# A fifth batch in seven block products: batch 4 of a conditioned two-layer residual kernel, with rank products and operand sums moved ahead

## The chip, the cores and the metric

The kernel runs on one core of a Trainium2 chip. The metric is device time in microseconds, the median of three runs. The profile is one further execution of the same program.

## The reference

Eight batches of x (1024 rows of 512) go through two layers, each with a residual. The first layer adds to its weight a product of rank 8 that is made from the batch's condition vector; the second scales its input columns by the condition and its output columns by a norm.

```python
xw = h @ w2 + b2                       # h = gelu(layernorm(cond) @ w1 + b1), a vector per batch
x_a, x_b = split(xw, 2)                # each (b, 512, 8)
layer = base_layer + einsum('bdr,bkr->bdk', x_a, x_b)
x = x + (x + einsum('btc,bco->bto', x, layer))
ys = cond / sqrt(512)
d = rsqrt(einsum('bi,io->bo', ys * ys, weight * weight) + 1e-8)
x = x + einsum('bsi,io->bso', x * ys, weight) * d
```

The two layers are linear in x, so per batch they are one 512 x 512 matrix, P, applied to x.

## The kernel before, in words

**Precision.** Each fp32 operand is held as two fp32r parts, high (rounded, copied by ScalarE: `x_high`, `q_high`, `r_high`) and low (the rest, subtracted by VectorE: `x_low`, `q_low`, `r_low`). A product takes three matmuls: high by high, high by low, low by high. All matmuls meant here are 128 x 128 by 128 x 512.

**P.** For batch b, P is base^T (w0, fixed) times a right factor r (built from w1, `ys` and `dinv` of the batch, by `r_scale`, `r_eye`, `r_high`, `r_low`, four chunks each) plus a product of rank 8 by 16 rows ("rank product", `rank`, one matmul for each of four chunks). Batches 0, 1 and 3 have their base tiles made early; 2 and 4 are made together as a pair in seven block products. All five are stored in `base` without the rank product, which TensorE writes to the four banks `ranks`, and VectorE adds it there (`p_sum`). For batches 5, 6 and 7 TensorE makes P late: four late tiles (`late_base`) of 12 matmuls and one rank product each, in the same four banks, between other work; ScalarE copies them out (`keep_late`). `rank_free` keeps TensorE from writing one of those banks before what was in it has been read: for a stored batch it waits for `p_summed` of the batch before.

**Applying P.** A plain batch takes two halves (h) of four tiles (o), each tile 4 x 3 matmuls over the chunks cc, so 96. A fast batch (those in `FAST`) is one Strassen-Winograd product: seven block products, the steps j of `STEPS`, each two tiles m of six matmuls, so 84. It needs from each operand four extra sums: of x (`x_sums_first`: three of them, t1, t3, t2; `x_sums_last`: t4), of P, called q here, (s1, s3, s2, s4). VectorE makes all of them. On the way out ScalarE evacuates banks 0 and 1 (`evacuate_block`, parts a, b, c, c12) and VectorE adds banks 2 and 3 (`finish_block`, blocks c11, c22, c21). A plain batch is evacuated by ScalarE alone. A bank is written anew only when it was read: `given` names for each step the block or part that must be out; step 6 waits for c22.

**Order.** Each engine runs its instructions in the order written; nothing else plans. While TensorE applies P to batch b, ScalarE and VectorE make the operands of batch n = b + 1 (`plain_batch`, `fast_batch` and, between two fast batches, `fast_pair`, in each engine's block). Buffers are rings: four slots for split x operands (`X_RING`), eight for q (`Q_RING`), six raw buffers for loaded quarters of x and the sum t2 (`RAW`). A slot is written when the matmuls of its former operand are done. SP's queue issues the loads of x (`load_x`) and some of the stores, in an order written out by hand; ScalarE's queue issues the other stores. GpSimd makes the masked left side of the rank products (`amk`, two buffers).

**Lines of the profile.** L1464 matmuls of a plain batch, L1495 of a fast one, L1323 late tiles, L1309 rank products; on VectorE L1000 low parts of x, L1069 low parts of q, L1012 to L1021 the sums of x, L1058 P's sums, L1105 `finish_block`, L930 a sum in the pair's preparation; on ScalarE L537 high parts of x, L566 high parts of q, L591 and L606 evacuations, L713 a scaling of r.

## Time and profile before

| | |
|---|---|
| median of 3 runs | 287.53 us (287.08 to 288.37) |
| profiled execution: device time | 287.95 us |
| its span, first to last instruction | 286.2 us |
| TensorE with work | 281.4 us, 98% |
| VectorE busy | 228.1 us, 80% |
| ScalarE busy | 170.1 us, 59% |
| granted TensorE clock, mean | 0.999 |

Matmuls are pipelined, and one's duration in the trace (0.39 us) is longer than the distance to the next. So TensorE's time is read from starts: where instructions of a line are merged, their number and the start of the next line give the distance. Durations of neighbouring VectorE instructions overlap a little in the same way. The time in brackets in an order of time is how long the engine was idle before the line, and for whom.

### The profile page before, as it was taken

Reading aid. Unit: us, or ns where it says so; the run is one execution under the profiler, and the core shown is the slowest. Engines: PE = TensorE matmul, PEld = TensorE weight load, DVE = VectorE, ACT = ScalarE, POOL = GpSimd, SP = SyncE. Lnnn points to the kernel's source line nnn. Section 1 sums busy time; section 2 is a strip of 40 time slices with the busy share of each in tenths; the row PEclk is TensorE's granted clock in tenths of the full one; section 3 lists DMA queues with packets and bytes.
Section 4 is the critical chain, followed back from the end, with each engine's and each line's share of the span. In section 5 each row is a group of like instructions: output and inputs, shape, how many; then the busy total and the mean of one; then the engine's idle time right before and its main releaser. Section 6 shows DMA issues by size and latency. Waiting matters only on the chain.

```text
span 286.2 us, 3812 instructions
## 1 busy us (share of the span) xinstructions
PE 281.4 (98%) x1368; PEld 222.0 (78%) x1368; DVE 228.1 (80%) x341; ACT 170.1 (59%) x260; POOL 18.6 (6%) x35
## 2 busy tenths in 40 slices
PE   8999999999999999999999999999999999999994
PEld 8778374756788888888888888888888888888783
DVE  3979969936688999984899978766787998987972
ACT  4757865530653648863648865534785587743771
POOL 5000000000520211000211000020000000000000
PEclk9999999999999999999999999999999999999999
DMA  6999797978044113499313499201134152371105
GB/s 187 372 425 422 290 421 297 419 302 324 2 147 147 76 74 128 165 279 407 123 79 142 149 301 419 89 0 74 73 114 182 74 179 116 101 266 73 53 23 220
DMA packets 13697, 55.31 MB, mean 193 GB/s; under 512 B 1776, under 2 KB 1776, under 8 KB 11376
## 3 DMA queue, kind: packets, MB, share of 16 engines
q1 hardware_dynamic: 10800, 45.64, 42.7%
q10 hardware_dynamic: 2880, 9.44, 8.3%
q8 instruction: 11, 0.18, 0.3%
q14 instruction: 6, 0.05, 0.1%
HBM read 38.30 MB, written 16.78 MB: 192 GB/s over the span
## 4 chain that ended last, share of the span: by engine, by line
PE 98%; DVE 0%; issue 0%; POOL 0%; POOLq 0%
PE tile L1495 33%; PE tile L1464 23%; PE tile L1384 7%; PE aux L1323 6%; PE acc L1255 5%; PE tile L1287 4%; PE tile L1270 4%; PE tile L1430 4%; PE spare L1323 3%; PE acc L1323 3%; PE tile L1226 2%; PE aux L1309 1%; PE aux L1233 1%; PE aux L1400 1%; PE spare L1309 1%; PE acc L1309 1%
## 5 line engine op out<-in xcount | busy, mean ns | idle before, releaser
L1495 PE MATMUL tile<-xs,qs 128*128 128x512 f32 x420 | 97.4, 390 | 0.0
L1495 PEld LDWEIGHTS tile<-xs,qs 128*128 128x128 f32 x420 | 78.7, 188 | 17.0 <-issue 0.7
L1464 PE MATMUL tile<-xs,qs 128*128 128x512 f32 x288 | 68.2, 389 | 0.0
L1464 PEld LDWEIGHTS tile<-xs,qs 128*128 128x128 f32 x288 | 54.1, 188 | 11.2
L1000 DVE TENSOR_TENSOR xs<-stream,xs 128x1024 fp32r<-128x1024 f32 x33 | 40.0, 1221 | 10.3 <-ACT xs L537 10.0
L537 ACT CAST xs<-stream 128x1024 fp32r<-128x1024 f32 x33 | 34.3, 1049 | 4.3 <-ACT stream L591 1.9
L606 ACT ACTIVATE stream<-tile,dts 128x512 f32<-128x512 f32 x40 | 26.6, 687 | 12.3 <-PE tile L1495 12.1
L591 ACT ACTIVATE stream<-tile,dts 128x512 f32<-128x512 f32 x24 | 16.4, 688 | 27.9 <-PE tile L1464 27.9
L1069 DVE TENSOR_TENSOR qs<-base,qs 128x512 fp32r<-128x512 f32 x38 | 25.0, 685 | 4.1 <-ACT qs L566 4.1
L1105 DVE SCALAR_TENSOR_TENSOR stream<-tile,dts,stream 128x512 f32<-128x512 f32 x30 | 21.9, 747 | 6.1 <-PE tile L1495 4.3
L417 POOL TENSOR_SCALAR amk<-asq,mask 128x512 fp32r<-128x512 f32 x8 | 14.3, 1794 | 172.9 <-PE spare L1309 98.9
L566 ACT CAST qs<-base 128x512 fp32r<-128x512 f32 x38 | 22.3, 620 | 4.3 <-DVE base L1165 1.9
L433 ACT CAST rs<-rtmp 128x512 fp32r<-128x512 f32 x24 | 14.7, 620 | 12.1 <-DVE rtmp L830 11.9
L1000 DVE TENSOR_TENSOR xs<-xr,xs 128x1024 fp32r<-128x1024 f32 x14 | 17.0, 1221 | 4.0 <-ACT xs L537 3.9
L1323 PE MATMUL aux<-rs,w0s 128*128 128x512 f32 x72 | 17.3, 389 | 0.0
L835 DVE TENSOR_TENSOR rs<-rtmp,rs 128x512 fp32r<-128x512 f32 x24 | 16.5, 687 | 0.8 <-ACT rs L433 0.4
L1323 PEld LDWEIGHTS aux<-rs,w0s 128*128 128x128 f32 x72 | 13.5, 188 | 2.8
L537 ACT CAST xs<-xr 128x1024 fp32r<-128x1024 f32 x14 | 14.6, 1049 | 0.5 <-ACT stream L606 0.5
L1430 PE MATMUL tile<-rs,w0s 128*128 128x512 f32 x48 | 12.1, 393 | 0.0
L1270 PE MATMUL tile<-rs,w0s 128*128 128x512 f32 x48 | 12.0, 401 | 0.0
L1287 PE MATMUL tile<-rs,w0s 128*128 128x512 f32 x48 | 11.5, 394 | 0.1
L1287 PEld LDWEIGHTS tile<-rs,w0s 128*128 128x128 f32 x48 | 8.9, 188 | 3.1 <-issue 1.3
(170 smaller groups left out, 324.2 us busy)
## 6 DMA issues: line engine op xcount, KB each, us to landing
...
```

The costliest lines, as they stand in the source:

```text
L537: nc.scalar.copy(x_slot(b, x)[:, 0], x_raw(b, home)).then_inc(x_hi, 1)
L566: nc.scalar.copy(to, src).then_inc(p_hi, 1)
L606: nc.scalar.activation(pairs[:, slot, m], tiles[m][:], ACT.Copy, scale=dts[:, b, o:o + 1]).then_inc(bank_free, 1)
L1000: nc.vector.tensor_tensor(x_slot(b, x)[:, 1], x_raw(b, home), x_slot(b, x)[:, 0].bitcast(F32), ALU.subtract).then_inc(x_lo, 1)
L1069: nc.vector.tensor_tensor(to, src, hi, ALU.subtract).then_inc(p_lo, 1)
L1105: nc.vector.scalar_tensor_tensor(to, tiles[2 + m][:], dts[:, b, o:o + 1], to, ALU.mult, ALU.add).then_inc(block_out, 1)
L1270: last = nc.tensor.matmul(tiles[cc][:], w0s[:, u, kc, cc * P:(cc + 1) * P], rs[:, kc, v], start=kc == 0 and (u, v) == (0, 0), stop=kc == K ...
L1287: last = nc.tensor.matmul(tiles[cc][:], w0s[:, u, kc, cols], rs[:, kc, v], start=kc == 0 and (u, v) == (0, 0), stop=kc == KC - 1 and (u, v ...
L1323: last = nc.tensor.matmul(ranks[cc][:], w0s[:, u, kc, cols], rs[:, kc, v], start=kc == 0 and (u, v) == (0, 0), stop=False)
L1430: last = nc.tensor.matmul(tiles[cc][:], w0s[:, u, kc, cols], rs[:, kc, v], start=kc == 0 and (u, v) == (0, 0), stop=False)
L1464: last = nc.tensor.matmul(tiles[o][:], q_slot(b, cc)[:, u, cols], x_slot(b, (h, cc // 2))[:, v, cc % 2], start=cc == 0 and (u, v) == (0, 0 ...
L1495: last = nc.tensor.matmul(tiles[bank + m][:], q_slot(b, q)[:, u, cols], x_slot(b, x)[:, v, k], start=opens and k == 0 and (u, v) == (0, 0) ...
```

## The change

- Batch 4 joins `FAST`. It is multiplied in seven block products, with its operand sums, and its finished blocks by VectorE.
- The sums of x are additions now (b11 + b12, b12 + b22, their sum with b22, and b21 with that), and the signs that this turns are turned back on the way out: parts c and c12 and block c22 are scaled by `dts_neg`, the negated `dts`. The sums of q become a22 - a21, a11 - a21, and two three-operand instructions for s2 and s4.
- Rank products: those of batch 3 go behind steps 3 to 6 of batch 1, those of batch 4 behind the first four tiles of batch 2. P's sums of batch 2 go to the start of batch 1, those of batches 3 and 4 are both made in batch 2.
- The q sums of batch 4 are made in batch 2, three of them in the still unused place of batch 5 in `base` (`AHEAD`, `q_src`).
- The right factor of batch 5 (the sixth) is built before and in batch 0. Its four late tiles go behind steps 0 to 3 of batch 4, those of batch 6 behind steps 3 to 6 of batch 5 (`LATE_STEP`). ScalarE makes the first two scalings of the factors of batches 6 and 7 at the end of the batch before.
- Raw buffers are given out by a table in the order in which they come free, and a fast batch loads its third quarter, (1, 0), first.

The diff, cut to its core:

```diff
-FAST = (1, 3, 5, 6, 7)
+FAST = (1, 3, 4, 5, 6, 7)
...
-LATE_STEP = {6: 1, 7: 3}
+
+LATE_STEP = {5: 0, 6: 3, 7: 3}
+AHEAD = {"s2": 1, "s1": 2, "s4": 3}
...
             if b in FAST:
-                raw_no[b, "sum"] = len(raw_used)
-                raw_used.append(x_op[b, "t2"] + 1)
+                b12, b11, b21, t2, b22, left = comes_free
+                homes = {(1, 0): b12, (0, 0): b11, (0, 1): b21, "sum": t2, (1, 1): b22}
+                comes_free = [left, t2, b12, b11, b22, b21]
+            else:
+                homes = {(h, cp): comes_free[2 * h + cp] for h in range(HALVES) for cp in range(2)}
+                comes_free = comes_free[4:] + comes_free[:4]
+            for home, at in homes.items():
+                raw_at[b, home], raw_after[b, home] = at, had[at]
+                had[at] = x_op[b, X_LAST[home] if b in FAST else home] + 1
+                if home != "sum":
+                    loads[at] += 1
+                    raw_loads[b, home] = loads[at]
 
...
+        def q_src(b, q):
+
+            if b == STORED - 1 and q in AHEAD:
+                return base[:, STORED - 1, AHEAD[q]].rearrange("p (k n) -> p k n", k=2)
+            return q_raw(b, Q_HOME[q])
...
-                paired = b - 1 in FAST and b in FAST
+                quarters = X_LOADS[b not in FAST]
                 if b - 2 in FAST and b - 1 in FAST:
                     store_block(b - 2, "c21", 1)
-                load_x(b, 0, 0)
+                load_x(b, *quarters[0])
+                load_x(b, *quarters[1])
                 if b - 1 in FAST:
                     store_block(b - 1, "c11", 0)
-                load_x(b, 0, 1)
-                if b - 2 in FAST and b - 1 not in FAST:
+                elif b - 2 in FAST:
                     store_block(b - 2, "c21", 1)
-                load_x(b, 1, 0)
-                if paired:
-                    load_x(b, 1, 1)
+                load_x(b, *quarters[2])
+                load_x(b, *quarters[3])
...
+            def r_scaled_ahead(b, kc):
+                act.wait_ge(r_lo, NO[b] * KC + kc + 1 - RTMP)
+                nc.scalar.activation(rtmp[:, kc % RTMP], w1s[:, kc], ACT.Copy,
+                                     scale=ys[:, b, kc:kc + 1]).then_inc(r_scaled, 1)
...
             pair_evacuate("c12", 5, 0, 1)
+            r_scaled_ahead(STORED, 0)
+            r_scaled_ahead(STORED, 1)
+            r_high(NO[STORED], 0)
+            r_scaled_ahead(STORED, 2)
...
+                    by = dts_neg if name in ("c", "c12") else dts
                     nc.scalar.activation(pairs[:, slot, m], tiles[m][:], ACT.Copy,
-                                         scale=dts[:, b, o:o + 1]).then_inc(bank_free, 1)
+                                         scale=by[:, b, o:o + 1]).then_inc(bank_free, 1)
...
                 evacuate_block(b, "a", 0, 0, 0)
+                if n == STORED:
+                    keep_late(n, (0,))
                 x_high(b, "t3")
...
+                elif n == STORED:
+                    x_high(b, "t1")
+                    keep_late(n, (1,))
+                    evacuate_block(b, "b", 2, 1, 1)
+                    q_high(b, "s4")
                 else:
                     q_high(b, "s4")
                     x_high(b, "t1")
                 q_high(b, "a22")
-                if n == B or b - 1 not in FAST:
+                if n == STORED:
+                    keep_late(n, (2,))
+                elif n == B or n < STORED:
                     evacuate_block(b, "b", 2, 1, 1)
                 x_high(b, "b22")
-                if n in FAST and LATE_STEP[n] == 1:
-                    keep_late(n, (0,))
-                    x_high(b, "t4")
-                    keep_late(n, (1,))
-                    q_high(n, "a11")
+                x_high(b, "t4")
+                if n not in FAST:
...
+                if n <= STORED:
+                    if n < STORED:
+                        q_high(n, "a11")
                     x_high(n, "b11")
-                    keep_late(n, (2,))
+                    if n == STORED:
+                        keep_late(n, (3,))
+                        q_high(n, "a11")
                     evacuate_block(b, "c", 4, 2, 1)
                     x_high(n, "b21")
-                    keep_late(n, (3,))
                     q_high(n, "a12")
                     evacuate_block(b, "c12", 5, 3, 0)
                     store_last_quarter(b)
                     x_high(n, "t2")
-                    q_high(n, "s2")
-                    q_high(n, "s3")
-                    q_high(n, "s1")
-                    for kc in range(RTMP):
-                        act.wait_ge(r_lo, NO[n + 1] * KC + kc + 1 - RTMP)
-                        nc.scalar.activation(rtmp[:, kc], w1s[:, kc], ACT.Copy,
-                                             scale=ys[:, n + 1, kc:kc + 1]).then_inc(r_scaled, 1)
-                    return
-                x_high(b, "t4")
-                if n in FAST:
+                else:
                     keep_late(n, (0,))
                     evacuate_block(b, "c", 4, 2, 1)
...
+                q_high(n, "s2")
+                q_high(n, "s3")
+                q_high(n, "s1")
+                if STORED <= n < B - 1:
+                    r_scaled_ahead(n + 1, 0)
+                    r_scaled_ahead(n + 1, 1)
...
+            nc.vector.tensor_scalar(dts_neg[:], dts[:], -1.0, None, ALU.mult).then_inc(dts_turned, 1)
+            dve.wait_ge(dts_turned, 1)
...
 
             def x_sums_first(b):
+
                 n = 4 * FAST.index(b)
-                b11, b12, b22, t2 = [x_raw(b, k) for k in ((0, 0), (1, 0), (1, 1), "sum")]
-                dve.wait_ge(x_loaded[raw_no[b, (1, 0)] % RAW], 16 * raw_loads[b, (1, 0)])
-                nc.vector.tensor_tensor(b11, b12, b11, ALU.subtract).then_inc(x_stepped, 1)
-                dve.wait_ge(x_loaded[raw_no[b, (1, 1)] % RAW], 16 * raw_loads[b, (1, 1)])
-                nc.vector.tensor_tensor(b12, b22, b12, ALU.subtract).then_inc(x_stepped, 1)
+                b11, b12, b22 = [x_raw(b, k) for k in ((0, 0), (1, 0), (1, 1))]
+                dve.wait_ge(x_lo, x_op[b, "b11"] + 1)
+                raw_loaded(dve, b, (1, 0))
+                nc.vector.tensor_tensor(b11, b11, b12, ALU.add).then_inc(x_stepped, 1)
+                raw_loaded(dve, b, (1, 1))
                 dve.wait_ge(x_stepped, n + 1)
-                nc.vector.tensor_tensor(t2, b22, b11, ALU.subtract).then_inc(x_stepped, 1)
+                nc.vector.tensor_tensor(b12, b12, b22, ALU.add).then_inc(x_stepped, 1)
+                if raw_after[b, "sum"]:
+                    dve.wait_ge(x_lo, raw_after[b, "sum"])
+                nc.vector.tensor_tensor(x_raw(b, "sum"), b11, b22, ALU.add).then_inc(x_stepped, 1)
 
...
                 dve.wait_ge(x_stepped, 4 * FAST.index(b) + 3)
-                nc.vector.tensor_tensor(b21, b21, t2, ALU.subtract).then_inc(x_stepped, 1)
+                dve.wait_ge(x_lo, x_op[b, "b21"] + 1)
+                nc.vector.tensor_tensor(x_raw(b, (0, 1)), x_raw(b, (0, 1)), x_raw(b, "sum"),
+                                        ALU.add).then_inc(x_stepped, 1)
+
+            def q_sums_first(b):
+
+                a11, a21, a22 = [q_raw(b, k) for k in ((0, 0), (1, 0), (1, 1))]
+                nc.vector.tensor_tensor(q_src(b, "s1"), a22, a21, ALU.subtract).then_inc(q_stepped, 1)
+                nc.vector.tensor_tensor(a21, a11, a21, ALU.subtract).then_inc(q_stepped, 1)
+
+            def q_sums_last(b):
+
+                n = 4 * FAST.index(b)
+                a11, a12 = q_raw(b, (0, 0)), q_raw(b, (0, 1))
+                dve.wait_ge(q_stepped, n + 1)
+                nc.vector.scalar_tensor_tensor(q_src(b, "s2"), q_src(b, "s1"), -1.0, a11, ALU.mult,
+                                               ALU.subtract).then_inc(q_stepped, 1)
+                dve.wait_ge(q_stepped, n + 3)
+                nc.vector.scalar_tensor_tensor(q_src(b, "s4"), a12, -1.0, q_src(b, "s2"), ALU.mult,
+                                               ALU.subtract).then_inc(q_stepped, 1)
...
             columns(dib, dinv).then_inc(cols_ready, 1)
+            r_eye(NO[STORED], 0)
+            r_eye(NO[STORED], 1)
             fix_first(0)
+            r_low(NO[STORED], 0)
             dve.wait_ge(c_halved, 1)
             nc.vector.tensor_tensor(ct, aux[1][0:64, :], c_part, ALU.add).then_inc(c_step, 1)
             dve.wait_ge(c_hi, 1)
             nc.vector.tensor_tensor(csp[64:128, :], ct, csp[0:64, :].bitcast(F32), ALU.subtract).then_inc(c_lo, 1)
+            r_eye(NO[STORED], 2)
             fix_first(1)
...
+                if b == 0:
+                    r_low(NO[STORED], 1)
+                    r_low(NO[STORED], 2)
                 x_low(b, (1, 1))
                 if b == 0:
+                    r_eye(NO[STORED], 3)
                     fix_first(2)
+                    r_low(NO[STORED], 3)
                     fix_first(3)
-                if STORED <= n < B:
-                    r_build(NO[n])
-                    if n not in FAST:
-                        for cc in range(KC):
-                            q_low(n, cc)
-                elif n < STORED:
+                for cc in range(KC):
+                    p_sum(n, cc)
+                q_first(n)
+                if b > 0:
+                    q_low(n, "s2")
+                    q_low(n, "s3")
                     for cc in range(KC):
-                        p_sum(n, cc)
-                if n in FAST:
-                    fast_operands(n)
-                    if n + 1 < STORED:
-                        for cc in range(KC):
-                            p_sum(n + 1, cc)
-                    elif n + 1 < B:
-                        r_build(NO[n + 1])
-                elif n < B:
-                    for cp in range(2):
-                        x_low(n, (0, cp))
-                        if n < STORED:
-                            q_low(n, 2 * cp)
-                            q_low(n, 2 * cp + 1)
+                        p_sum(n + 1, cc)
+                x_low(n, "b11")
+                x_low(n, "b21")
+                x_sums(n)
+                if b == 0:
+                    q_low(n, "s2")
+                    q_low(n, "s3")
+                else:
+
+                    q_sums_first(n + 1)
+                    q_sums_last(n + 1)
...
-                if LATE_STEP[n] == 1:
+                if n < STORED:
                     q_low(n, "a11")
                     x_low(n, "b11")
                     x_sums_first(n)
                     finish_block(b, "c22", 3, "c", 2, 1)
+                    x_low(n, "b21")
+                    x_sums_last(n)
+                    q_low(n, "a12")
+                    finish_block(b, "c21", 6, "b", 1, 1)
+                    x_low(n, "t2")
+                elif n == STORED:
+                    x_low(n, "b11")
+                    x_sums_first(n)
+                    dve.wait_ge(late_kept, late_fast(n))
+                    q_low(n, "a11")
+                    finish_block(b, "c22", 3, "c", 2, 1)
+                    x_low(n, "b21")
+                    x_sums_last(n)
+                    q_sums_first(n)
+                    q_low(n, "a12")
+                    q_sums_last(n)
+                    finish_block(b, "c21", 6, "b", 1, 1)
+                    x_low(n, "t2")
                 else:
                     finish_block(b, "c22", 3, "c", 2, 1)
                     x_low(n, "b11")
                     q_low(n, "a11")
                     x_sums_first(n)
...
+                    x_low(n, "b21")
+                    x_sums_last(n)
                     finish_block(b, "c21", 6, "b", 1, 1)
                     x_low(n, "t2")
...
+                    dve.wait_ge(late_kept, late_fast(n))
+                    q_sums_first(n)
+                    q_low(n, "a12")
+                    q_sums_last(n)
                 q_low(n, "s2")
                 q_low(n, "s3")
...
                 if b - 1 not in FAST:
+                    if n not in FAST:
+                        p_sum(n, 0)
+                        p_sum(n, 1)
                     x_low(b, "t2")
                     q_low(b, "s1")
-                if n < B and b - 1 in FAST:
+                if STORED < n < B:
                     r_eye(NO[n], 0)
                     r_eye(NO[n], 1)
                 finish_block(b, "c11", 1, "a", 0, 0)
+                if n < B and n not in FAST:
+                    p_sum(n, 2)
+                    p_sum(n, 3)
                 x_low(b, "t3")
-                if n < B and b - 1 in FAST:
+                if STORED < n < B:
...
             def rank_free(b, cc):
 
-                if b > STORED and b - 1 in FAST:
+                if b > STORED:
                     pe.wait_ge(late_kept, late_fast(b - 1) - KC + cc + 1)
-                elif b > STORED:
-                    pe.wait_ge(p_lo, q_op[b - 1, cc] + 1)
                 elif b > 1:
                     pe.wait_ge(p_summed, keep(b - 1, cc))
...
+                        if b == 0:
+                            rank(h + 1, o)
+                        elif h == 0:
                             rank(n + 1, o)
-                    if h == 0 and STORED <= n < B:
-                        for cc in range(KC):
-                            late_base(n, cc)
...
+                    if n not in FAST and n < B and j >= len(STEPS) - KC:
+                        rank(n + 1, j + KC - len(STEPS))
                     if STORED <= n < B and 0 <= j - LATE_STEP[n] < KC:
                         late_base(n, j - LATE_STEP[n])
```

## Rows read from the trace of the kernel before

**Rows 1.** Page: TensorE's work, and the shares of the chain that ended last.

```profile
PE 281.4 (98%) x1368; PEld 222.0 (78%) x1368; DVE 228.1 (80%) x341; ACT 170.1 (59%) x260; POOL 18.6 (6%) x35
...
PE 98%; DVE 0%; issue 0%; POOL 0%; POOLq 0%
```

**Rows 2.** Stretches of batches 1 and 5: length, busy us (instructions) of TensorE, weight loads, VectorE, ScalarE, GpSimd; clock, DMA share, GB/s.

```profile
106.03:125.07 19.04, 19.04 (x85) 15.77 (x84) 18.58 (x25) 16.10 (x23) 2.19 (x1) 1.00 0.45 158
...
201.23:232.06 30.83, 30.83 (x138) 25.53 (x136) 25.46 (x33) 20.67 (x30) 0.00 (x0) 1.00 0.30 116
```

**Rows 3.** Order of time, TensorE: start, duration, what; batches 1, 2 and 7.

```profile
106.03 19.20 PE L1495 MATMUL tile<-xs,qs 128*128 128x512 f32 x84
...
124.85 2.68 PEld L1464 LDWEIGHTS tile<-xs,qs 128*128 128x128 f32 x12
...
125.07 2.88 PE L1464 MATMUL tile<-xs,qs 128*128 128x512 f32 x12
...
262.88 19.66 PE L1495 MATMUL tile<-xs,qs 128*128 128x512 f32 x84
```

**Rows 4.** Order of time, VectorE, before and in batch 0.

```profile
72.95 0.68 DVE L1042 TENSOR_TENSOR stream<-aux,stream 64x512 f32<-64x512 f32 x1 [2.53 <-ACT stream L574]
...
87.04 1.23 DVE L1000 TENSOR_TENSOR xs<-stream,xs 128x1024 fp32r<-128x1024 f32 x1 [1.59 <-ACT xs L537]
```

**Rows 5.** Waits: engine and line, for whom, us in total, times, longest.

```profile
ACT stream L574 <- PE aux L1405: 7.8, 1, 7.8
```

**Rows 6.** Order of time, VectorE, end of batch 0 and batch 1.

```profile
101.24 1.22 DVE L1012 TENSOR_TENSOR stream<-xr,stream 128x1024 f32<-128x1024 f32 x1
...
105.91 1.29 DVE L1069 TENSOR_TENSOR qs<-base,qs 128x512 fp32r<-128x512 f32 x2
...
107.11 1.28 DVE L1058 TENSOR_TENSOR base<-aux,base 128x512 f32<-128x512 f32 x2
...
111.24 1.41 DVE L1105 SCALAR_TENSOR_TENSOR stream<-tile,dts,stream 128x512 f32<-128x512 f32 x2
...
112.56 1.22 DVE L1000 TENSOR_TENSOR xs<-xr,xs 128x1024 fp32r<-128x1024 f32 x1
```

**Rows 7.** Loads of x (L332): from issue to landing.

```profile
DMA to landing us min/median/max: 3.0/4.4/8.9
```

**Rows 8.** Order of time, ScalarE and VectorE, batch 2.

```profile
128.58 1.04 ACT L537 CAST xs<-xr 128x1024 fp32r<-128x1024 f32 x1
...
129.65 1.23 DVE L1000 TENSOR_TENSOR xs<-xr,xs 128x1024 fp32r<-128x1024 f32 x1 [2.14 <-ACT xs L537]
...
130.79 1.28 DVE L1058 TENSOR_TENSOR base<-aux,base 128x512 f32<-128x512 f32 x2
```

**Rows 9.** Order of time, VectorE, batch 3.

```profile
158.67 2.36 DVE L1000 TENSOR_TENSOR xs<-stream,xs 128x1024 fp32r<-128x1024 f32 x2
...
160.94 1.29 DVE L1069 TENSOR_TENSOR qs<-base,qs 128x512 fp32r<-128x512 f32 x2
...
162.15 0.75 DVE L1105 SCALAR_TENSOR_TENSOR stream<-tile,dts,stream 128x512 f32<-128x512 f32 x1
```

**Rows 10.** Order of time, ScalarE, batch 5.

```profile
218.26 1.05 ACT L537 CAST xs<-stream 128x1024 fp32r<-128x1024 f32 x1 [1.52 <-PE tile L1495]
```

**Rows 11.** Order of time, VectorE, the pair's preparation.

```profile
43.14 1.68 DVE L930 SCALAR_TENSOR_TENSOR rtmp<-w1s,ys,base 128x256 f32<-128x256 f32 x4
```

**Rows 12.** Order of time, ScalarE and weight loads, batches 6 and 7.

```profile
233.21 1.33 ACT L713 ACTIVATE rtmp<-w1s,ys 128x512 f32<-128x512 f32 x2
...
267.81 1.26 ACT L606 ACTIVATE stream<-tile,dts 128x512 f32<-128x512 f32 x2
...
268.60 13.52 PEld L1495 LDWEIGHTS tile<-xs,qs 128*128 128x128 f32 x60 [0.32 <-issue]
```

**Rows 13.** Stretches of the tail, columns as in rows 2.

```profile
282.50:284.00 1.50, 0.05 (x1) 0.00 (x0) 0.75 (x1) 0.00 (x0) 0.00 (x0) 1.00 0.59 224
...
285.50:286.20 0.70, 0.00 (x0) 0.00 (x0) 0.00 (x0) 0.00 (x0) 0.00 (x0) 0.62 0.00 0
```

198 lines of the change are left out of this document (72 added, 126 removed).

## The prediction

> **What bounds the kernel now.** I read the page first: TensorE has work during 98% of the span, and the chain that ended last runs through TensorE alone [rows 1]. The table by batch says the same: TensorE fills each stretch at the full clock, while VectorE fills 98% of batch 1 and 83% of batch 5 [rows 2]. So the time is the number of matmuls by their pitch, plus any wait of TensorE. The pitch comes from TensorE's order of time: the 84 matmuls of batch 1 take 19.04 us from their start to batch 2's [rows 3]. One takes 0.2267 us, a group of 12 (a step of a fast batch, called 0 to 6 here) 2.72, a rank product 0.23, a late tile 2.95. Only batch 7 has 0.46 us more (19.66 against 19.20) [rows 3]: the one place where a wait shows. So the change gains only what it takes off TensorE, and pays for each operand that VectorE or ScalarE brings late. With VectorE this full, the place of each instruction in its queue decides.
>
> VectorE's pitches, as differences of starts: low part of x 1.135 us, low part of q 0.605 [rows 9], P's sum the same 0.6, one half of a finished block 0.66, four x sums 4.67 [rows 6]. A result is seen some 0.09 after the next start (durations overlap by so much), and TensorE's first matmul starts 0.22 after its weight load [rows 3].
>
> **What it removes.** Batch 4 goes from 8 x 4 x 3 = 96 matmuls to 84; rank products and late tiles stay in number. 12 x 0.2267 = 2.72 us less. VectorE gets for batch 4 three low parts of x and of q, four x sums, four q sums and six halves of blocks, and gives six scalings to ScalarE.
>
> **What costs nothing.** Batch 5's right factor is built around batch 0. ScalarE's additions fall into its 7.8 us wait [rows 5], VectorE's into 2.53 us of idle time before batch 0 and 1.59 us in it [rows 4]; without that cover they are four low parts of 0.6 and four eyes of about 0.27 on VectorE, 3.5 us. The rank products of batch 3, moved behind steps 3 to 6 of batch 1, find their banks free (P's sums of batch 2 end by 113.6, the first is due at 116.9). In batch 4 ScalarE keeps each late chunk behind q sums that lie in that chunk's place; they were read off early in batch 4, apart from s4, due only by chunk 3. The negated table is one small operation. The new order of x loads frees nothing that is waited for now: the view of waits names no x load. A landing takes 3.0 to 8.9 us, 4.4 at the middle [rows 7]. On SP's queue the stores now stand around these loads in another order, but the fourth quarter, which matters below, is issued when its buffer falls free, with its store behind it.
>
> **Batch 1, t3.** P's sums of batch 2 stood behind batch 1's operands; now two are ahead of t2 and two ahead of t3. The second half of c11 starts when step 1 is done: 106.03 + 5.44 + 0.2 = 111.67. Then 0.66 for it, 1.2 for two sums and 1.22 for t3's low part give 114.75, the matmul 114.97. Step 3 wants it at 106.03 + 3 x 2.72 = 114.19. Cost 0.8 (0.5 to 0.9). Today t3 is started at 112.56 [rows 6].
>
> **Batch 2, first rank product of batch 4.** This is the largest term. The product now follows tile 0 of batch 2 and writes a bank that still holds batch 3's rank product, so `rank_free` waits for P's sum of batch 3, chunk 0. VectorE reaches that sum behind both low parts of batch 2's second half, and the second of them waits for ScalarE's high part, which is queued behind the evacuation of tile 0. Today this very sum starts at 130.79 [rows 8], 5.72 us after the batch (125.07), and takes 0.68. Nothing ahead of it changes. It ends at 6.40 and TensorE goes on at 6.65, where it wants to at 2.72: cost 3.9 (3.7 to 4.1). In TensorE's queue tiles 1 to 7 stand behind the wait, and ScalarE waits for those tiles, so nothing catches up. Chunks 1 to 3 are in time (the next sum ends at 7.0, wanted at 9.6).
>
> **Batch 3, finish of c22.** Batch 4 is now fast, so behind t4 VectorE takes the low parts of a11 and b11 and three x sums before c22. Today two low parts of q stand between (160.94 to 162.15) [rows 9]: c22 starts 13.5 us into the batch (start 148.65), and step 6, which writes its bank, is due at 16.32. On the new path t4 ends at 12.05 (12.29 today, less 0.24, since TensorE's step 1 now sets c11's start). 12.05 + 0.6 + 1.135 + 3.5 = 17.3, + 0.75 for c22's first half + 0.22 = 18.27. Cost 1.95. The second x sum also needs batch 4's fourth quarter, whose buffer falls free with b22 at 11.0: landed at 14.0 by the shortest, at 15.4 by the median [rows 7], wanted at 15.0. So 1.7 to 2.4; I take 2.0. The q sums of batch 4 that VectorE makes in batch 2 (2.6 us) add nothing, for c11's wait lies between.
>
> **Batches 4 and 5.** In batch 4 a late tile follows each of steps 0 to 3, and VectorE idles there. The high part of batch 5's b11 needs the ring slot of t3, free 19.72 + 0.2 us into batch 4, and takes 1.05 (as at 218.26 today [rows 10]). From 21.07 on VectorE has until t3 of batch 5: three low parts of x 3.4, four x sums 4.65, five low parts of q 3.0, four q sums 2.65, six halves of blocks 4.0, two eyes 0.5, and t3's 1.22: 19.4, so 40.5. TensorE wants the weight load at 30.83 + 8.16 - 0.22 = 38.77. Cost 1.8, a part of it already at step 1 through c21. If the fourth quarter lands after the median instead of the shortest time, 1.1 more; if the sums overlap better than I add, 0.5 less. So 1.3 to 2.9; I take 2.0. Today the late tiles stand behind steps 1 to 4, which leaves VectorE 3 us more after that slot.
>
> The q sums s2 and s4 turn from plain subtractions into three-operand instructions with two fp32 tensors. The trace has that form with 256 columns: 4 in 1.68 us, 0.48 for one, so a pitch of 0.40 [rows 11]. 256 columns more cost half of what 512 more cost between low parts of q and x (0.53), 0.27: 0.66, used above. The Trainium skill (Vector Engine (DVE) Microarchitecture Reference, Points that are easy to get wrong) says that this form has half the throughput when its two SBUF sources are not bf16. By that rule one of 512 columns would take some 1.2 us and the sum rise by about 2.2 (batches 1, 5, 6). The row speaks against it: a column costs 0.53 / 512, so 256 at half rate would need 0.53 us, more than the whole instruction takes.
>
> **Batch 6, evacuation of a.** The pattern of batches 6 to 7 is now used for 5 to 6 too. Today ScalarE, behind s2, s3 and s1, evacuates a at 267.81, and step 2's weight load comes 0.32 late [rows 12]. The change puts two scalings (1.33 less the overlap, 1.24) ahead of that evacuation. Cost in batch 6: 0.46 + 1.24 + 0.06 for s2's new form = 1.8; VectorE's eyes and t3 lie under it. If some slack is left, 1.3. Batch 7 keeps its 0.46.
>
> **Sum.** -2.7 + 0.8 + 3.9 + 2.0 + 2.0 + 1.8 = +7.8. The profiled execution took 287.95 us (span 286.2, 1.75 around it): 295.7. The median of the runs is 287.53: 295.3. I say 295.5. The terms' ends add to +5.8 and +9.4: 293.3 to 297.0.
>
> **Rivals.**
> 1. The clock falls in batch 2's gap. In the tail, with no matmul since 282.54, the granted clock is still full at first and 0.62 in the last 0.7 us: at 1.2 GHz for most of that stretch [rows 13]. Batch 2's gap would be 3.7 us long. No row shows how long matmuls would then run at twice the pitch; for as long as the gap or twice as long they lose 1.8 to 3.7: 297.1 to 299. Against it: I see one fall only. Chance 0.15. The Trainium skill (TensorE: Matmul & The Clock Gate, Why this matters for your kernels) warns against such idle gaps between bursts of matmuls; the tail agrees.
> 2. Only batch 2's wait is real; at the other places, which rest on my adding up VectorE's queue, a microsecond or two of slack hides the rest. 287.5 - 2.7 + 3.9, plus 0 to 2: 288.7 to 291. Chance 0.13.
> 3. Faster: P's sum of batch 3 reaches the bank before the rank product, because ScalarE's and VectorE's first work in batch 2 starts earlier than today's (it hangs on tile 0's evacuation, so I don't see how). Below a wait of 2.7 minus the other terms the sign turns; with none of them 284.8, with half 287.7. Chance 0.07 for faster, 0.04 for no change.
> 4. It does nothing, since TensorE isn't the limit and 12 matmuls fewer shorten nothing: 287.5. The gapless 19.04 us speak against it. 0.01.
>
> The forecast has 0.60. The range from 291.0 to 298.3 takes in half of rival 1 and leaves out rival 3 and nearly all of rival 2. A difference under 0.5% (1.4 us) can't be told from none: faster 0.07, same 0.06, slower 0.87.
>
> **What would show it.** Batch 2's first rank product starts 6.6 us into the batch, released by VectorE's sum. Step 3 of batch 1 waits for t3, step 6 of batch 3 for c22, steps 1 to 3 of batch 5 for VectorE, step 2 of batch 6 for ScalarE's evacuation. Batch 4's 136 matmuls take 30.8 us without a gap. The prediction is wrong if that first rank product is not late, or if VectorE idles where I have it full.

## The result, and the profile after

| | before | after |
|---|---|---|
| median | 287.95 us (287.08 to 290.74, 4 runs) | 299.39 us (297.66 to 299.89, 4 runs) |
| ratio | | 1.037, 95% interval 1.0286 to 1.0453 |
| profiled execution | 287.95 us, span 286.2 | 299.57 us, span 297.8 |
| mean granted clock, profiled execution | 0.999 | 0.989 |

The change costs 4%, 11.4 us. The direction was forecast, but the time is 3.9 us above the forecast of 295.5 and 1.1 us above the range's upper end of 298.3.

The page of the kernel after answers to [rows 1]:

```profile
PE 283.7 (95%) x1356; PEld 220.7 (74%) x1356; DVE 243.2 (82%) x356; ACT 178.1 (60%) x272; POOL 18.6 (6%) x35
...
PEclk9999999999999999997999979999999999999999
...
PE 80%; DVE 14%; issue 3%; ACT 2%; DVEq 0%; POOL 0%; ACTq 0%; POOLq 0%
```

TensorE has 12 matmuls fewer, yet 2.3 us more of work. It was busy during 98% of the span and is now at 95%, and a seventh of the chain that ended last is VectorE's. The clock line has two slices at 0.7, which the kernel before doesn't have. So there are two kinds of loss, waits and slow matmuls.

TensorE's order of time in the kernel after shows both. The idle time and its releaser are in brackets. This answers to [rows 3].

```profile
105.91 8.32 PE L1541 MATMUL tile<-xs,qs 128*128 128x512 f32 x36
115.08 3.01 PE L1541 MATMUL tile<-xs,qs 128*128 128x512 f32 x12 [0.85 <-DVE xs L1027]
...
127.00 2.88 PE L1513 MATMUL tile<-xs,qs 128*128 128x512 f32 x12
133.45 0.50 PE L1358 MATMUL aux<-csq,amk 128*128 128x512 f32 x1 [3.57 <-DVE base L1111]
133.79 4.51 PE L1513 MATMUL tile<-xs,qs 128*128 128x512 f32 x12
138.14 0.40 PE L1358 MATMUL aux<-csq,amk 128*128 128x512 f32 x1
...
155.17 16.48 PE L1541 MATMUL tile<-xs,qs 128*128 128x512 f32 x72
173.82 7.35 PE L1541 MATMUL tile<-xs,qs 128*128 128x512 f32 x24 [2.17 <-DVE stream L1140]
181.01 2.88 PE L1372 MATMUL aux<-rs,w0s 128*128 128x512 f32 x12
...
200.96 11.04 PE L1541 MATMUL tile<-xs,qs 128*128 128x512 f32 x48
213.01 5.72 PE L1541 MATMUL tile<-xs,qs 128*128 128x512 f32 x24 [1.01 <-DVE stream L1140]
219.50 3.03 PE L1541 MATMUL tile<-xs,qs 128*128 128x512 f32 x12 [0.76 <-DVE xs L1027]
...
249.28 5.72 PE L1541 MATMUL tile<-xs,qs 128*128 128x512 f32 x24 [1.15 <-ACT stream L643]
```

Every wait of the forecast is there, at the place and with the releaser that it named. What it didn't have is the duration of two groups. The 13 matmuls from 133.45 to 138.14 take 4.69 us where 13 x 0.2267 is 2.95, and the 24 from 173.82 to 181.01 take 7.19 where 5.44 is normal. The stretches around these two places have the columns of [rows 2]; the third number from the end is the granted clock:

```profile
129.88:133.45 3.57, 0.00 (x0) 0.00 (x1) 1.88 (x3) 1.62 (x2) 0.00 (x0) 1.00 0.98 330
133.45:138.14 4.69, 4.69 (x13) 3.68 (x14) 3.03 (x5) 0.00 (x0) 0.00 (x0) 0.64 0.39 145
...
171.80:173.82 2.02, 0.00 (x0) 0.03 (x1) 2.02 (x4) 1.35 (x2) 0.00 (x0) 1.00 0.29 120
173.82:176.00 2.18, 2.18 (x8) 1.77 (x9) 2.08 (x3) 1.84 (x4) 0.00 (x0) 0.82 0.69 280
176.00:178.00 2.00, 2.00 (x6) 1.54 (x6) 2.00 (x3) 0.00 (x0) 0.00 (x0) 0.50 0.24 98
```

In both gaps the granted clock is still full; it falls to 0.50, the lower of its two levels, only after the matmuls have begun again. Reading the clock of the idle stretch alone would say that nothing happened. At 0.50 a matmul takes 0.427 us instead of 0.2267 (12 in 5.12 us, in the c22-first experiment below), 1.9 times as long. The Trainium skill (TensorE: Matmul & The Clock Gate, Why this matters for your kernels) warns of long idle gaps between bursts of matmuls. The rows of batch 2 agree; batch 3's gap of 2.17 us is shorter than those that it warns of, and the measurement decides: slow matmuls stand behind it too.

By batches, from start to start, against matmuls times 0.2267:

| batch | length | without waits | more | of it waits | of it clock | forecast |
|---|---|---|---|---|---|---|
| 1 | 21.09 | 19.95 | 1.1 | 1.1 | | 0.8 |
| 2 | 28.17 | 22.67 | 5.5 | 3.7 | 1.7 | 3.9 |
| 3 and 4 | 53.95 | 49.87 | 4.1 | 2.3 | 1.8 | 2.0 |
| 5 | 33.19 | 30.83 | 2.4 | 2.4 | | 2.0 |
| 6 | 32.47 | 30.83 | 1.6 | 1.6 | | 1.8 |
| sum | | | 14.7 | 11.2 | 3.5 | 10.5 |

Less the 2.7 us of the 12 matmuls that is 12.0; the two profiled executions differ by 11.6. The other 0.4 us lie outside these batches: in the kernel after, batch 1 starts 0.1 us sooner, and from the start of batch 7 to the end it is 0.3 us shorter (23.02 for 23.32). Why was not looked into. The other three runs of the kernel after had a mean clock of 0.987, 0.989 and 0.993, and the one with 0.993 is the fastest, 297.66 us.

VectorE's order of time in the kernel after names who is late. In batch 2, answering to [rows 8]:

```profile
131.57 1.23 DVE L1027 TENSOR_TENSOR xs<-stream,xs 128x1024 fp32r<-128x1024 f32 x1 [2.47 <-ACT xs L566]
132.71 1.28 DVE L1111 TENSOR_TENSOR base<-aux,base 128x512 f32<-128x512 f32 x2
...
169.32 1.23 DVE L1040 TENSOR_TENSOR xr<-xr,stream 128x1024 f32<-128x1024 f32 x1
...
171.80 1.22 DVE L1046 TENSOR_TENSOR xr<-xr,stream 128x1024 f32<-128x1024 f32 x1
172.93 1.41 DVE L1140 SCALAR_TENSOR_TENSOR stream<-tile,dts_neg,stream 128x512 f32<-128x512 f32 x2
```

The sum that frees the bank starts 5.71 us into batch 2 (forecast 5.72), behind a low part of x that waited 2.47 us for ScalarE although the sum needs nothing of it. The lower rows are batch 3: c22 (L1140) starts 17.8 us into the batch, after three sums of x that only batch 4 needs. TensorE had run out at 171.49 (155.17 + 72 x 0.2267).

### The profile page after: what moved, and what is told of

It reads as the page before. It is cut to its first block, busy times and chain, and to the rows that moved or that the text cites. A ratio compares the mean times of both kernels' runs of the same rounds, so it can differ in the third digit from the quotient of the medians.

```text
span 297.8 us, 3851 instructions
## 1 busy us (share of the span) xinstructions
PE 283.7 (95%) x1356; PEld 220.7 (74%) x1356; DVE 243.2 (82%) x356; ACT 178.1 (60%) x272; POOL 18.6 (6%) x35
## 4 chain that ended last, share of the span: by engine, by line
PE 80%; DVE 14%; issue 3%; ACT 2%; DVEq 0%; POOL 0%; ACTq 0%; POOLq 0%
PE tile L1541 28%; PE tile L1513 11%; PE tile L1433 7%; PE aux L1372 5%; PE acc L1306 5%; PE tile L1321 4%; PE tile L1338 4%; DVE xs L1027 4%; PE tile L1479 4%; PE spare L1372 3%; PE acc L1372 3%; DVE stream L1140 2%; DVE qs L1122 2%; PE tile L1277 2%; DVE base L1111 2%
## 5 line engine op out<-in xcount | busy, mean ns | idle before, releaser
L1541 PE MATMUL tile<-xs,qs 128*128 128x512 f32 x504 | 120.8, 395 | 5.9 <-DVE stream L1140 3.2
L1513 PE MATMUL tile<-xs,qs 128*128 128x512 f32 x192 | 47.3, 399 | 0.0
L1027 DVE TENSOR_TENSOR xs<-stream,xs 128x1024 fp32r<-128x1024 f32 x29 | 35.2, 1228 | 6.0 <-ACT xs L566 5.8
L1122 DVE TENSOR_TENSOR qs<-base,qs 128x512 fp32r<-128x512 f32 x41 | 27.4, 696 | 11.3 <-ACT qs L592 11.3
L566 ACT CAST xs<-stream 128x1024 fp32r<-128x1024 f32 x29 | 29.8, 1046 | 0.5 <-ACT stream L643 0.5
L592 ACT CAST qs<-base 128x512 fp32r<-128x512 f32 x41 | 24.0, 619 | 8.3 <-DVE base L1066 6.5
L627 ACT ACTIVATE stream<-tile,dts 128x512 f32<-128x512 f32 x16 | 11.0, 689 | 25.0 <-PE tile L1513 24.9
L1027 DVE TENSOR_TENSOR xs<-xr,xs 128x1024 fp32r<-128x1024 f32 x21 | 25.5, 1219 | 0.4
L1140 DVE SCALAR_TENSOR_TENSOR stream<-tile,dts,stream 128x512 f32<-128x512 f32 x24 | 17.3, 746 | 8.4 <-PE tile L1541 8.0
L566 ACT CAST xs<-xr 128x1024 fp32r<-128x1024 f32 x21 | 22.0, 1051 | 2.8 <-ACT stream L627 0.9
L643 ACT ACTIVATE stream<-tile,dts_neg 128x512 f32<-128x512 f32 x24 | 16.3, 688 | 8.8 <-PE tile L1541 8.8
L643 ACT ACTIVATE stream<-tile,dts 128x512 f32<-128x512 f32 x24 | 15.6, 682 | 7.8 <-PE tile L1541 7.8
L1372 PE MATMUL aux<-rs,w0s 128*128 128x512 f32 x72 | 17.3, 389 | 0.0
```

The costliest lines, as they stand in the source:

```text
L566: nc.scalar.copy(x_slot(b, x)[:, 0], x_raw(b, home)).then_inc(x_hi, 1)
L592: nc.scalar.copy(to, src).then_inc(p_hi, 1)
L643: nc.scalar.activation(pairs[:, slot, m], tiles[m][:], ACT.Copy, scale=by[:, b, o:o + 1]).then_inc(bank_free, 1)
L1027: nc.vector.tensor_tensor(x_slot(b, x)[:, 1], x_raw(b, home), x_slot(b, x)[:, 0].bitcast(F32), ALU.subtract).then_inc(x_lo, 1)
L1122: nc.vector.tensor_tensor(to, src, hi, ALU.subtract).then_inc(p_lo, 1)
L1140: nc.vector.scalar_tensor_tensor(to, tiles[2 + m][:], by[:, b, o:o + 1], to, ALU.mult, ALU.add).then_inc(block_out, 1)
```

## The experiments

The table splits the 14.7 us into waits and slow matmuls; what causes each is still argued only. **Theory:** the places in VectorE's and ScalarE's queues make the waits, and the two longest waits each cost another 1.7 us, because the clock falls behind them. **Rival:** the engines have too much work, so that a wait taken away at one place comes back at the next; and the slow matmuls come from something else, such as VectorE or the DMAs, which move more in those stretches.

**Batch 2's sums first.** One part of the order is put right: VectorE makes P's sums of batch 3 ahead of both low parts of x.

```diff
             def plain_batch(b):
                 n = b + 1
+                if b > 0:
+                    for cc in range(KC):
+                        p_sum(n, cc)
                 x_low(b, (1, 0))
...
-                for cc in range(KC):
-                    p_sum(n, cc)
+                if b == 0:
+                    for cc in range(KC):
+                        p_sum(n, cc)
```

> VectorE makes P's sums of batch 3 at the start of batch 2, ahead of both low parts of x. Theory (the sum of waits, each with its own place): TensorE's 3.6 us gap before the first rank product of batch 4 goes, and with it the half-rate matmuls behind it (13 matmuls in 4.69 us instead of 2.95, 1.7 us). 3.7 + 1.7 = 5.4 us less than the changed kernel, about 294.0 us. Rival (the waits are one shortage of VectorE, which turns up at the next place when one is mended): the time falls by 2 us or less, and the gaps in batches 3 and 5 grow. Rival (the slow matmuls come from traffic, not from the gap): 3.7 us less, 295.7.

Measured 293.66 us (292.88 to 293.72), ratio 1.0188 (1.0169 to 1.0207): 5.7 less than the changed kernel. Batch 2 has no gap, and no wait came back behind it. In VectorE's order of time of this kernel the low part of x behind the sums now waits 0.33 us for ScalarE, not 2.47: the sums fill time that VectorE had spent waiting.

```profile
127.38 1.28 DVE L1111 TENSOR_TENSOR base<-aux,base 128x512 f32<-128x512 f32 x2
...
131.32 1.22 DVE L1027 TENSOR_TENSOR xs<-stream,xs 128x1024 fp32r<-128x1024 f32 x1 [0.33 <-ACT xs L566]
```

Its TensorE still shows batch 3's gap of 2.18 us, and the slow 24 matmuls behind it. So the second fall of the clock needs no first one. It did not come in every run, as far as the mean clock tells: three of the four have 0.994, the fastest (292.88 us) has 0.998.

```profile
168.07 7.31 PE L1545 MATMUL tile<-xs,qs 128*128 128x512 f32 x24 [2.18 <-DVE stream L1140]
```

**c22 first.** The other part of the order alone: in batch 3 VectorE finishes c22 before the x sums of batch 4.

```diff
                     x_low(n, "b11")
-                    x_sums_first(n)
                     finish_block(b, "c22", 3, "c", 2, 1)
+                    x_sums_first(n)
```

> In batch 3 VectorE finishes c22 before the three x sums of batch 4, nothing else is changed. Theory: the 2.2 us wait of step 6 goes, and the 1.7 us of half-rate matmuls behind it: 3.9 us less, 295.5 us, while the gap in batch 2 stays at 3.6. Rival (one shortage of VectorE): c21's finish and batch 4's steps come late instead, under 1.5 us less. Rival (no clock loss through a gap of only 2.2 us): 2.3 less, 297.1.

Measured 297.26 us (296.39 to 297.80), ratio 1.0317 (1.0293 to 1.0340): 2.1 less than the changed kernel, where 3.9 were expected. The time alone would fit the rival that the gap of 2.2 us cost no clock (297.1). The rows decide against it: the gap in batch 3 is gone, with its slow matmuls, and batches 3 and 4 take 49.87 us (157.09 to 206.96) for 53.95, 4.1 less. Of the 1.8 us that are missing in the total, 1.2 are in batch 2, whose gap is as long as before but cost more, and 0.7 lie before batch 1, which starts at 106.60 for 105.91. (Over the eleven profiled executions this start lies between 105.18 and 107.87; so much of a difference in time can be chance, and lengths of batches tell more.) TensorE's rows, then two stretches:

```profile
134.18 0.79 PE L1358 MATMUL aux<-csq,amk 128*128 128x512 f32 x1 [3.57 <-DVE base L1111]
134.78 5.32 PE L1513 MATMUL tile<-xs,qs 128*128 128x512 f32 x12
...
157.09 21.92 PE L1541 MATMUL tile<-xs,qs 128*128 128x512 f32 x96
```

```profile
130.00:134.18 4.18, 0.61 (x3) 0.19 (x1) 1.88 (x3) 1.62 (x2) 0.00 (x0) 0.91 1.00 336
134.18:140.29 6.11, 6.11 (x14) 4.79 (x15) 3.04 (x5) 0.15 (x1) 0.00 (x0) 0.50 0.30 111
```

Here the clock was already down at the end of the gap (0.91 over the stretch) and stayed at 0.50 for 14 matmuls: 6.11 us for 14 x 0.2267 = 3.17, a loss of 2.9 where the changed kernel's profiled execution lost 1.7. (The first 12 behind the rank product take 5.12 us, 134.78 to the next rank product at 139.90.) The same gap in the same place has no fixed price.

**Gaps filled.** Both waits stay, but TensorE runs 14 matmuls in the one and 8 in the other, all into banks that are overwritten next. So work and waits of the other engines should stay as they were.

```diff
                         elif h == 0:
+                            if o == 0:
+                                bank_ready(b, 1, 0)
+                                for _ in range(14):
+                                    nc.tensor.matmul(tiles[1][:], q_slot(b, 0)[:, 0, 0:P], x_slot(b, (0, 0))[:, 0, 0],
+                                                     start=True, stop=True)
                             rank(n + 1, o)
...
+                            if (b, j, m) == (3, 6, 0):
+                                pe.wait_ge(p_summed, keep(STORED - 1, KC - 1))
+                                for _ in range(8):
+                                    nc.tensor.matmul(ranks[0][:], q_slot(b, q)[:, 0, 0:P], x_slot(b, x)[:, 0, 0],
+                                                     start=True, stop=True)
                             pe.wait_ge(block_out, dve_no[b, given[j], m])
```

> Both waits stay; while they last TensorE does matmuls whose results nobody reads: 14 in batch 2 before the rank product, 8 in batch 3 before the second-bank tile of step 6 (3.2 and 1.8 us of work). Theory (idle TensorE lets the clock fall): the granted clock stays full and the matmuls behind the gaps run at 2.72 us per 12: 3.4 us less with 22 matmuls more, 296.0 us. Rival (the slow stretches come from something else, such as transfers or VectorE's traffic at that time): no change, 299.4, or slower.

Measured 296.38 us (296.03 to 296.52), ratio 1.0291 (1.0274 to 1.0308), mean clock 1.000 in every run: 22 matmuls more and 3.0 us less. TensorE's rows show the rank product 6.45 us into batch 2, just as late as without the filling, and the matmuls behind both places at full pace. Last comes the stretch behind the rank product:

```profile
126.92 2.88 PE L1513 MATMUL tile<-xs,qs 128*128 128x512 f32 x12
129.64 3.33 PE L1524 MATMUL tile<-xs,qs 128*128 128x512 f32 x14
133.37 0.50 PE L1358 MATMUL aux<-csq,amk 128*128 128x512 f32 x1 [0.40 <-DVE base L1111]
...
169.78 1.98 PE L1545 MATMUL aux<-xs,qs 128*128 128x512 f32 x8
172.02 5.78 PE L1551 MATMUL tile<-xs,qs 128*128 128x512 f32 x24 [0.27 <-DVE stream L1140]
```

```profile
133.37:138.04 4.67, 4.67 (x20) 3.86 (x21) 3.04 (x5) 0.92 (x2) 0.00 (x0) 1.00 0.43 152
```

That settles the second kind of loss: the idle gaps of TensorE cause the slow matmuls. VectorE's and the DMAs' work behind the gap is what it was (3.04 us and a share of 0.43 here, 3.03 and 0.39 in the changed kernel), and the clock is 1.00 where it had been 0.64.

**Both orders right.** The first two edits together.

> The edits of the first two experiments together. Theory: their gains add, 5.4 + 3.9 = 9.3 us less, 290.1 us, mean clock back at 0.999; what is left over the kernel before is 1.1 + 2.4 + 1.6 us of waits in batches 1, 5 and 6 less 2.7 for the 12 matmuls. Rival (one shortage): the sum is at most 6 us less, 293 or more.

Measured 290.17 us (289.87 to 290.43), ratio 1.0073 (1.0057 to 1.0089), clock 0.998 to 1.000: 9.2 us less than the changed kernel. The sum of the two waits (3.7 + 2.3) and the two slow stretches (3.5) is 9.5. Both orders of VectorE and what the clock made of them were four fifths of the 11.4 us. The waits of batches 1, 5 and 6 stay as they were: 0.87, 1.01 and 0.77, and 1.16 us idle.

**t3 and the scalings.** On top of the last: t3's low part ahead of P's two sums in batch 1, and ScalarE's two scalings ahead of its copies of s2, s3 and s1, so that neither stands before the evacuation of a.

```diff
+                if STORED <= n < B - 1:
+                    r_scaled_ahead(n + 1, 0)
+                    r_scaled_ahead(n + 1, 1)
                 q_high(n, "s2")
                 q_high(n, "s3")
                 q_high(n, "s1")
-                if STORED <= n < B - 1:
-                    r_scaled_ahead(n + 1, 0)
-                    r_scaled_ahead(n + 1, 1)
...
                 finish_block(b, "c11", 1, "a", 0, 0)
+                x_low(b, "t3")
                 if n < B and n not in FAST:
                     p_sum(n, 2)
                     p_sum(n, 3)
-                x_low(b, "t3")
```

> The kernel with both orders of VectorE mended (290.2 us), and two more: in batch 1 VectorE makes t3's low part ahead of the last two of P's sums of batch 2, and ScalarE makes the two scalings for the next right factor ahead of its copies of s2, s3 and s1. If order within the queue is all that is wrong there, the 1.1 us of batch 1 and the 1.2 us of batch 6 go: 287.9 us. Rival: VectorE has too much work in batch 1 whatever the order, and the wait of step 3 comes back at a later step (s4 or a22), so only batch 6 gains: 289.0. Second rival: the scalings ahead hold up s2 and s3 at the head of batches 5 and 6 and nothing is gained there: 289 to 290.

Measured 288.39 us (287.46 to 290.08, 13 runs), ratio 1.0009 (0.9990 to 1.0027). The profiled execution is the slowest of the 13 (290.08); its batch 1 starts 1.6 us later than the last kernel's. Batch 1 takes 20.00 us (107.87 to 127.87 in its order of time), gapless: its 1.1 are gone. Batch 6, from 233.61 to 265.39, is 0.7 shorter, of the 1.6 that it had too much: where step 2 had waited for ScalarE, step 3 now waits for VectorE (0.78 us from start to start, part of it before steps 1 and 2).

```profile
233.61 8.72 PE L1545 MATMUL tile<-xs,qs 128*128 128x512 f32 x36
242.55 3.06 PE L1545 MATMUL tile<-xs,qs 128*128 128x512 f32 x12 [0.22 <-DVE xs L1027]
...
265.39 19.65 PE L1545 MATMUL tile<-xs,qs 128*128 128x512 f32 x84
```

**All four late tiles moved.** From here on it is batch 5's 2.4 us. This kernel has both orders right, and batch 5's late tiles behind steps 1 to 4 of batch 4, as the kernel before has those of batch 6 in batch 5.

```diff
-LATE_STEP = {5: 0, 6: 3, 7: 3}
+LATE_STEP = {5: 1, 6: 3, 7: 3}
...
                     x_high(n, "b11")
+                    evacuate_block(b, "c", 4, 2, 1)
                     if n == STORED:
                         keep_late(n, (3,))
                         q_high(n, "a11")
-                    evacuate_block(b, "c", 4, 2, 1)
```

> The kernel with both orders of VectorE mended (290.2 us), and batch 5's late tiles behind steps 1 to 4 of batch 4 instead of 0 to 3, with ScalarE's evacuation of c ahead of its last late chunk. If batch 5 waits because the ring slot of t3 came free late, VectorE starts 3 us sooner on batch 5's operands and the 2.4 us of batch 5 go: 287.8 us. Rival: VectorE's amount of work, not the slot, sets it, or the last late chunk is now what it waits for; then 289.5 to 290.2, or more, with a wait of VectorE for the late chunks in the trace.

Measured 293.88 us (293.71 to 294.46), ratio 1.0216 (1.0197 to 1.0234): a miss, 3.7 us slower than without the move. TensorE's rows, then one of ScalarE and two of VectorE, in its batch 4 (which starts at 168.57):

```profile
172.45 3.00 PE L1545 MATMUL tile<-xs,qs 128*128 128x512 f32 x12 [0.99 <-DVE stream L1140]
...
200.37 5.71 PE L1545 MATMUL tile<-xs,qs 128*128 128x512 f32 x24 [2.25 <-DVE stream L1140]
207.29 5.72 PE L1545 MATMUL tile<-xs,qs 128*128 128x512 f32 x24 [1.21 <-DVE stream L1140]
```

```profile
189.82 0.59 ACT L653 COPY base<-acc 128x512 f32<-128x512 f32 x1 [2.88 <-PE acc L1362]
```

```profile
191.39 2.36 DVE L1027 TENSOR_TENSOR xs<-stream,xs 128x1024 fp32r<-128x1024 f32 x2 [2.51 <-ACT xs L566]
...
199.48 1.40 DVE L1140 SCALAR_TENSOR_TENSOR stream<-tile,dts_neg,stream 128x512 f32<-128x512 f32 x2
```

Two new waits. With no late tile between steps 0 and 1, step 1 of batch 4 no longer has 2.95 us of cover for c21, and waits 0.99. And I had moved the late tiles but not ScalarE's first three copies of them: the third copy waits 2.88 us for its later tile, with the high parts of b22, t4 and b11 queued behind it. So VectorE starts on them 22.8 us into the batch (18.8 with the tiles unmoved), and c22, behind the sums again, is 2.25 us late for step 6. A tile that moves on one engine has to be moved in the queue of each engine that reads it.

**All of these together.**

> All of these mendings together: 285.4 us, if the waits were independent: the kernel before (287.9 to 288) less the 12 matmuls of batch 4 (2.7). Rival: VectorE, now with hardly any idle time from batch 3 to 6, lets a wait come back at another step: 286.5 to 288.

Measured 291.93 us (291.30 to 292.65), ratio 1.0145 (1.0123 to 1.0167): a miss too, 6.5 us above the 285.4 expected, with the same two waits. It shows one more thing of the clock. First TensorE's rows of its batches 4 and 5, then the stretch behind the gap, and last the same stretch of the kernel with only the late tiles moved, whose gap is the same 2.25 us:

```profile
198.65 12.74 PE L1545 MATMUL tile<-xs,qs 128*128 128x512 f32 x48 [2.25 <-DVE stream L1140]
```

```profile
198.65:204.50 5.85, 5.85 (x19) 4.70 (x20) 5.71 (x8) 2.05 (x4) 0.00 (x0) 0.72 0.39 159
```

```profile
200.37:205.81 5.44, 5.44 (x24) 4.39 (x24) 5.30 (x8) 0.40 (x2) 0.00 (x0) 1.00 0.42 171
```

The clock fell at the one gap and not at the other. That is a matter of the execution more than of the kernel: of the four runs with only the tiles moved two have a mean clock of 0.999 and 1.000 and two have 0.994; the four of this kernel have 0.994 or 0.992. And where it fell, the wait for c21 at batch 5's step 1 (1.21 us in the kernel with only the tiles moved) is not there: the slow matmuls made TensorE late by about 1.6 and VectorE caught up meanwhile. From step 6 of batch 4 to step 3 of batch 5 one kernel takes 13.39 us (198.65 to 212.04), the other 13.40 (200.37 to 213.77): here the fall cost nothing. What a fall costs is what is left after such waits.

**Late tiles spread.** Both orders of VectorE right, t3 and the scalings as in the fifth kernel, and now the tiles behind steps 0, 2, 3 and 4: the first stays as cover for c21. ScalarE's copies move with them, and VectorE waits for the third and fourth chunk only behind c22.

```diff
-LATE_STEP = {5: 0, 6: 3, 7: 3}
+LATE_AT = {5: (0, 2, 3, 4), 6: (3, 4, 5, 6), 7: (3, 4, 5, 6)}
...
                     x_high(b, "t1")
-                    keep_late(n, (1,))
                     evacuate_block(b, "b", 2, 1, 1)
...
                 if n == STORED:
-                    keep_late(n, (2,))
+                    keep_late(n, (1,))
...
                     x_high(n, "b11")
                     if n == STORED:
-                        keep_late(n, (3,))
                         q_high(n, "a11")
+                        keep_late(n, (2,))
                     evacuate_block(b, "c", 4, 2, 1)
                     x_high(n, "b21")
+                    if n == STORED:
+                        keep_late(n, (3,))
...
                     x_sums_first(n)
-                    dve.wait_ge(late_kept, late_fast(n))
+                    dve.wait_ge(late_kept, late_fast(n) - 2)
                     q_low(n, "a11")
                     finish_block(b, "c22", 3, "c", 2, 1)
                     x_low(n, "b21")
                     x_sums_last(n)
+                    dve.wait_ge(late_kept, late_fast(n))
```

> The kernel with both orders of VectorE, t3 and the scalings mended, and batch 5's late tiles behind steps 0, 2, 3 and 4 of batch 4: the first stays where it covers the finish of c21, and ScalarE's copies of the late chunks and VectorE's wait for them move behind b22, b11 and c22, so that neither queue waits for a late tile. Added up from starts: step 3 ends 16.8 us into batch 4 instead of 19.7, t3's low part of batch 5 is then about 0.3 late. So most of the 2.4 us of batch 5 go: 285.9 us, below the kernel before (288). Rival: VectorE's amount of work between step 3 of batch 4 and step 3 of batch 5, 19.4 us, is what sets it, and only 0.5 to 1 goes: 287 to 287.5. Second rival: a wait at another step of batch 4 takes its place, as when all four late tiles moved: 289 or more.

Measured 285.64 us (285.24 to 286.26, 6 runs; before 288.03, 17 runs), ratio 0.9898 (0.9863 to 0.9933): 1% faster than the kernel before, 13.8 us faster than the changed one. Its order of time, VectorE's b11 low part first, then TensorE's rows at the end of batch 4 and in batch 5:

```profile
185.90 1.22 DVE L1028 TENSOR_TENSOR xs<-xr,xs 128x1024 fp32r<-128x1024 f32 x1
```

```profile
193.14 16.48 PE L1547 MATMUL tile<-xs,qs 128*128 128x512 f32 x72
209.46 2.88 PE L1378 MATMUL aux<-rs,w0s 128*128 128x512 f32 x12
```

That low part starts 18.15 us into batch 4 (start 167.75); with both orders right alone it was 21.1. The 3 us are enough: steps 5 and 6 of batch 4 and steps 0 to 3 of batch 5, 72 matmuls, run in 16.32 us without a gap. So the amount of VectorE's work did not set batch 5; the start did.

What had held that start back is not told by this run alone, since it moves two things: the end of step 3, which frees the slot of t3, and ScalarE's copies. The rows of the kernel with both orders right have them side by side, ScalarE's high part of b11 first, then VectorE's low parts of b22 and t4:

```profile
189.02 1.05 ACT L566 CAST xs<-xr 128x1024 fp32r<-128x1024 f32 x1 [0.24 <-PE tile L1545]
```

```profile
187.86 2.36 DVE L1027 TENSOR_TENSOR xs<-stream,xs 128x1024 fp32r<-128x1024 f32 x2 [0.91 <-ACT xs L566]
```

ScalarE waits 0.24 us for the slot and is done at 190.07; but VectorE is busy with b22 and t4 until b11's low part follows at 190.14, and these two had waited for ScalarE, which stood at the copy of the third late tile (1.29 us idle at 186.30). The kernel with all four tiles moved tells the two causes apart: there the slot is free 18.0 us into batch 4, not 19.7, and yet b11's low part starts at 25.1, not 21.1. So with both orders right the slot and the copies in ScalarE's queue hold the start to the same moment, and freeing the slot alone gains nothing.

**12 matmuls more.** The same kernel with 12 matmuls added at the head of batch 4, whose result is overwritten.

> As the kernel with the late tiles spread, with 12 matmuls more at the head of batch 4, whose result is overwritten. If TensorE sets batch 4's time, each costs its 0.2267 us: 2.7 us more. If VectorE or ScalarE set batches 4 and 5, the 12 matmuls are covered in part by waits that shrink: less than 2 us more.

Measured 288.55 us (287.66 to 290.80, 12 runs), ratio 1.0010 (0.9983 to 1.0037): 2.9 us more than without them, and level with the kernel before. In the rows it is 2.72: from batch 4's start to batch 6's it takes 64.37 us (168.08 to 232.45) for 61.65 (167.75 to 229.40). So TensorE sets the time of the mended batches, and the 12 matmuls that the change saves are worth their 2.7 us once nothing waits.

## Why the prediction was wrong

**The step that failed** is the sum's silence on the clock. The terms priced only idle time and took TensorE to go on at 0.2267 us per matmul behind each gap. The runs showed two stretches at half rate, 1.7 us behind batch 2's gap and 1.8 behind batch 3's, 3.5 together; with the gaps filled they were gone. With them the forecast would have been 299. The waits themselves came to 11.2 for 10.5. Rival 1 named the mechanism and a price (1.8 to 3.7, from [rows 13]), but had a chance of 0.15 and counted one fall. Its reason against, that one fall only was to be seen, was no evidence about gaps in the middle: the kernel before has none there, and the forecast itself put one of 3.7 us in. For a gap of 2 us there was no row either way, which was a reason to let the range reach to two falls, not to leave the second out.

**12 matmuls less**: right, 2.7; the last experiment shows 2.9 in the medians and 2.72 in the rows.

**Batch 1, t3**: 1.1 for 0.8. Place and cause right (putting t3 first takes it away).

**Batch 2, rank product**: right, 3.7 for 3.9, and the largest term as said. Its full price was 5.5 with the clock.

**Batch 3, c22**: 2.3 for 2.0; I had c22 start 17.3 us into the batch, it was 17.8. With the clock 4.1.

**Batches 4 and 5**: 2.4 for 2.0. VectorE's late start, 21.1 us into batch 4, is as forecast, but the cause named for it, the slot of t3, is only one of two: ScalarE's copy of the third late tile, with b22 and t4 behind it, held it to the same moment (190.14 for 190.07). The prediction had listed these copies under what costs nothing; that its number came out in spite of that is luck. By the profile the fourth quarter's load played no part.

**Batch 6**: 1.6 for 1.8. Right cause; but taking it away gained 0.7 only, for step 3 came late instead.

**STT form**: the q sums' three-operand instructions take 0.68 to 0.69 us with 512 columns, the same as a plain one; the next start follows 0.61 us after the second (c21's, at 212.12) and 0.72 after the first, on whose result the second depends. The mean is what I took, 0.66. VectorE's rows in the kernel after:

```profile
210.19 0.68 DVE L1122 TENSOR_TENSOR qs<-base,qs 128x512 fp32r<-128x512 f32 x1
210.79 0.69 DVE L1066 SCALAR_TENSOR_TENSOR base<-q_sum,base 128x512 f32<-128x512 f32 x1
211.51 0.69 DVE L1069 SCALAR_TENSOR_TENSOR base<-base 128x512 f32<-128x512 f32 x1
```

The measurement decides against the Trainium skill's half throughput (Vector Engine (DVE) Microarchitecture Reference, Points that are easy to get wrong) for this form with two fp32 tensors in SBUF.

**The rivals**: rival 2 (only batch 2 real) fell, since no microsecond of slack hid the other places. Rival 3 fell, since the rank product was 3.7 us late; its 287.7 for half of the waits was also added up wrongly, for half of 10.5 on 284.8 is 290.1. Rival 4 fell, since the time rose. What the prediction costed at nothing, the sixth right factor around batch 0 and the order of loads, left no wait of TensorE there: batch 0 takes 23.58 us for 23.57.

**Open**: of the sums of x for batches 1 and 5 the second starts 1.68 us after the first, with 0.46 idle, though it waits for nothing but the first by the profile; for batches 3 and 4 the same pair starts 1.32 and 1.33 apart. No run was made for it. And what decides whether a gap of 2.2 us costs the clock was not found.
